# A transformer layer on one core: the order of all steps as a table, the last batch projected by head, the norms' roots as powers on POOL

## The reference

```
x = x + attn(layernorm(x))       # 16 heads, latent keys = values (72 wide), causal softmax,
                                 #   z[t, 16*72] @ out_w + out_b
x = x + birwkv(r = layernorm(x), k = v = ctx)
                                 # sigmoid(r) * (Af + Ab + cur*v) / (Bf + Bb + cur),
                                 #   A, B = forward and backward scans over the 128 tokens
x = x + moe(layernorm(x))        # 8 experts, top 2 of them per token, silu(x Wg) * (x Wu), then Wd
layernorm(x) = (x - mean) / sqrt(var + 1e-5)
```

## Time and profile before

| | us |
|---|---|
| median of 3 runs | 646.59 (645.44 to 647.18) |
| the profiled execution's own time | 645.62 |
| its span, from the first to the last instruction | 644.0 |
| PE busy | 549.7 (85%) |
| DVE busy | 427.3 (66%) |
| ACT busy | 367.4 (57%) |
| POOL busy | 341.5 (53%) |

### The profile page before, as it was taken

One profiled execution on the slowest core, in us unless ns is written; L12 is line 12 of the kernel. 1 busy time (PEld: TensorE's weight loads), 2 busy tenths in 40 slices (PEclk: granted clock), 3 DMA queues, 4 the chain that ended last, 5 costly groups with the idle time before them and its releaser, 6 DMA issues.

```text
span 644.0 us, 11145 instructions
## 1 busy us (share of the span) xinstructions
PE 549.7 (85%) x3714; PEld 480.9 (75%) x3714; DVE 427.3 (66%) x888; ACT 367.4 (57%) x995; POOL 341.5 (53%) x313
## 2 busy tenths in 40 slices
PE   1987688999898999999869757894799999999991
PEld 0875566778677888878648437784799999999991
DVE  4468485685888786846846858594477777777760
ACT  4276554676467765655553344563467667776750
POOL 3374757547372486623611742173766767665433
PEclk9999988999899999999878668797889999999997
DMA  6324444364354425443120277256668897888710
GB/s 208 126 47 71 61 86 62 51 84 74 56 98 85 70 44 74 95 88 61 44 92 22 93 224 256 61 113 187 155 155 238 221 237 204 230 224 224 174 28 0
DMA packets 54540, 76.04 MB, mean 118 GB/s; under 512 B 11410, under 2 KB 42899, under 8 KB 54227
## 3 DMA queue, kind: packets, MB, share of 16 engines
q1 hardware_dynamic: 43210, 63.32, 40.2%
q0 software_dynamic: 10384, 11.86, 9.7%
q10 hardware_dynamic: 888, 0.15, 0.1%
HBM read 49.03 MB, written 10.40 MB: 92 GB/s over the span
## 4 chain that ended last, share of the span: by engine, by line
PE 50%; DVE 16%; POOL 12%; issue 9%; ACT 7%; DMA 4%; SPq 0%; POOLq 0%; ACTq 0%; DVEq 0%
PE P L921 22%; PE PO L921 9%; PE PO L1031 5%; PE P L999 4%; PE P L1017 4%; POOL xs L1830 3%; ACT EB L1212 2%; POOL EB L1787 2%; DVE small L1450 2%; PE P L1007 2%; DVE ZT L1465 2%; DMA out<-Y,TK 1%; PE P L1069 1%; ACT XN L1173 1%; PE P L939 1%
## 5 line engine op out<-in xcount | busy, mean ns | idle before, releaser
L921 PE MATMUL P<-GT,WF 128*128 128x256 f32 x1104 | 149.3, 294 | 10.1 <-DVE GT L1362 6.0
L921 PEld LDWEIGHTS P<-GT,WF 128*128 128x128 f32 x1104 | 142.8, 201 | 11.3 <-DVE GT L1362 6.7
L1212 ACT ACTIVATE EB<-P,small 128x128 f32<-128x128 f32 x256 | 90.7, 367 | 97.1 <-DVE small L1450 96.9
L1787 POOL TENSOR_TENSOR EB<-EB,small 128x512 f32<-128x512 f32 x64 | 77.1, 1206 | 127.3 <-DVE small L1454 127.1
L1871 POOL DMA_INDIRECT out<-Y,TK x46 | 74.8, 1626 | 74.2 <-ACT Y L1301 56.3
L1017 PE MATMUL P<-PT,V 128*72 128x512 f32 x128 | 71.0, 639 | 18.0 <-DVE ZT L1465 16.6
L1844 POOL DMA_INDIRECT cxa<-xd,TK x46 | 62.2, 1353 | 39.7 <-DMA TK<-xs 29.0
L1031 PE MATMUL PO<-Ow,zP 128*128 128x256 f32 x288 | 73.4, 396 | 3.2 <-DMA zP<-ZT 1.9
L999 PEld LDWEIGHTS P<-KT,qT 72*128 72x128 f32 x512 | 68.9, 196 | 8.2 <-DMA qT<-qP 4.5
L999 PE MATMUL P<-KT,qT 72*128 72x128 f32 x512 | 69.6, 280 | 4.1 <-DMA qT<-qP 3.6
L921 PE MATMUL PO<-WF,HR 128*128 128x256 f32 x552 | 71.4, 287 | 0.0
(11 more groups left out here) (182 smaller groups left out, 930.9 us busy)
## 6 DMA issues: line engine op xcount, KB each, us to landing
WR<-wf SPq DMA_DIRECT2D x33, 512.0 KB, 4.9
arena<-wf SPq DMA_DIRECT2D x33, 512.0 KB, 5.0
qT<-qP SPq DMA_DIRECT2D x63, 128.0 KB
zP<-ZT SPq DMA_DIRECT2D x80, 72.0 KB
zP<-ZT SPq DMA_DIRECT2D x96, 36.0 KB
X<-x SPq DMA_DIRECT2D x4, 512.0 KB, 7.4
cxa<-ctxin SPq DMA_DIRECT2D x4, 512.0 KB, 6.8
out<-X SPq DMA_DIRECT2D x3, 512.0 KB, 4.3
```

The costliest lines, as they stand in the source:

```text
L921: r = e.matmul(o, lt(a), rt_(b), start=start and n == 0, stop=stop and n == 2, skip_group_check=skip)
L1212: e.activation(EB[i][:, j, :], S[:, 128 * j:128 * j + 128], ACT.Exp, bias=NM[i][:, j:j + 1], accum_out=SM[i][:, j:j + 1]).then_inc(s_exp, 1)
L1787: e.tensor_tensor(EB[i][:, :, :], EB[i][:, :, :], SM[i].unsqueeze(2).broadcast_to([128, 4, 128]), ALU.mult).then_inc(s_prob, 1)
```

## The change

Four things change together.

1. The planner is gone. ORDER is a table, STEPS, of words such as `S.5` or `rs.3.3.2.2`, up to tile 10; from there a loop emits the same pattern as before. Steps keep their content, but nearly all side steps move by some places. The output of a tile, on POOL, has a step of its own (`ao`) and no longer goes with `dn`.
2. The last batch (15) is not packed. SP loads a second copy of the output weights, ordered by head, into the query buffer 0 (`load_ow_by_head`, two DMAs, 1.18 MB), and `project_by_head` multiplies ZT with it: 4 matmuls of 72 rows after each of its four units, 16 in place of 9, in another quarter of the PSUM tensor PO.
3. All roots of the norms are one POOL instruction, `tensor_tensor(..., ALU.pow)` with -0.5. The 10 or 13 small operations go.
4. Waits that follow from the buffers: HR and the low half of the weights of tile 1, and the loads of tile 1, wait for the last projection.

```diff
-SHARE, SHARE_TILES = 0.7, 3.0
...
+STEPS = """
...
+S.63 Y.59 add.6 bn.2.3.0.0 ltk.3 agg.2.3.0.2 rs.2.3.0.2 N.62 N.63 T.60 gtk.0 Y.60 nr.3.0.2 sig.3.0.0 x2.3.0.0.1 gtk.1 O.14.0
...
+"""
-    def newton(kind, g, b0, nb, i):
...
             def pack_z(n):
                 k, b, hq = UNITS[n]
                 z, nb = packing(n)
-                if nb == 1 or b % NB == NB - 1:
+                if b < B - 1 and (nb == 1 or b % NB == NB - 1):
...
+            def load_ow_by_head():
+                sp.wait_ge(s_S, PER * (NK - 1))
+                by_head = ow.rearrange("p m c -> (p m) c").rearrange("(h l) c -> l h c", l=L)
+                e.dma_start(qT[0][:, 4:16, :], by_head[:, 0:12, :]).then_inc(s_owh, 16)
+                e.dma_start(qT[0][:, 0:4, :], by_head[:, 12:16, :]).then_inc(s_owh, 16)
...
+            def project_by_head(b, i):
+                n = 4 * b + i
+                buf, half, _ = z_home(n)
+                o = PO[:, 1, 256:512]
+                if i == 0:
+                    pe.wait_ge(s_owh, 32)
+                    pe.wait_ge(s_wk, total["wb"])
+                    pe.wait_ge(s_add, b // 2)
+                pe.wait_ge(s_z, n + 1)
+                for j in range(4):
+                    p = e.matmul(o, ZT[buf][:, j, 128 * half:128 * half + 128], ow_head(4 * i + j), start=4 * i + j == 0, stop=4 * i + j == H - 1)
+                p.then_inc(s_O, 1)
...
-                e.tensor_scalar(ve[:, 0:nb], mv[:, 0:nb, 1], EPS, -0.5, ALU.add, ALU.mult).then_inc(s_ve, 1)
+                e.tensor_scalar(ve[:, 0:nb], mv[:, 0:nb, 1], EPS, None, ALU.add).then_inc(s_ve, 1)
...
+            def rstd(kind, g, b0, nb):
+                y = rs1[:, GB * g:GB * g + GB] if kind == 1 else rs2
+                po.wait_ge(s_nhalf, 1)
+                po.wait_ge(s_ve, nth("agg", kind, g, b0, nb))
+                e.tensor_tensor(y[:, 0:nb], ve[:, 0:nb], nhalf[:, 0:nb], ALU.pow).then_inc(s_rstd, 1)
```

More of the change, by code:

```diff
@@ L73, in schedule @@
+tg.10 lw.12.1 sh.9.0 sh.9.1 lw.11.2 ao.7 sw.9.2 lxg.12
+"""
 def schedule():
-    order = []
+    order = [(name, *map(int, a)) for name, *a in (w.split(".") for w in STEPS.split())]
     def emit(*step):
[L78 to L241, removed]
@@ L272, in plan @@
[L272 to L291, removed]
@@ L318, in split_w @@
-    def split_w(j, k):
[L319 to L328, removed]
@@ L330, in turn @@
-    def turn(n, k=1):
-        for _ in range(k):
-            now[0] += 1
-            credit[0] = min(credit[0] + st["share"], st["share"] + 0.1)
-            for i, parts_ in enumerate(beside):
-                while credit[0] > 0 and parts_ and parts_[0][0] <= n and wake[i] <= now[0]:
-                    c = next(parts_[0][1], "end")
-                    if c == "end":
-                        parts_.pop(0)
-                    elif c is not None and c < 0:
-                        wake[i] = now[0] - c
-                    else:
-                        credit[0] -= c or 0.6
@@ L344, in finish @@
-    def finish(n, until):
-        st["rush"] = True
-        while not until():
-            assert any(p and p[0][0] <= n for p in beside)
-            for i, parts_ in enumerate(beside):
-                if parts_ and parts_[0][0] <= n and next(parts_[0][1], "end") == "end":
-                    parts_.pop(0)
-        st["rush"] = False
-    for p in (0, 2):
-        emit("bn", 1, 0, 0, p)
-    emit("agg", 1, 0, 0, GB, True)
-    for i in range(3):
-        emit("rs", 1, 0, 0, GB, i)
-    emit("nmb", 1, 0, 0, GB)
@@ L505, in schedule @@
-    for j in range(2, NT):
-        due = j + 1 < NT and not ready(j + 1)
-        def prepare(k):
-            if not due:
-                split_w(j + 1, k)
-        beside_turn(j + 3)
-        prepare(0)
-        product(j, 0)
-        beside_turn(j + 3)
-        if j + 1 < NT and not due:
-            emit("tg", j + 1)
-        beside_turn(j + 3)
-        prepare(1)
+        if step[1] < NT:
+            order.append(step)
+    def split_w(j, k):
+        emit("sw", j, k)
+        emit("lw", j + 2, k)
```

374 lines of the change are left out of this document (126 added, 248 removed).

## The result

The changed kernel takes 619.66 us (616.59 to 624.57, four runs), and the kernel before on the same chip 646.88 (645.44 to 647.82): a ratio of 0.9588, interval 0.9516 to 0.9661. On two more chips the same program gave 0.9683 (0.963 to 0.9737) and 0.9603 (0.9562 to 0.9645); taken together that is some 0.962, or 24 us. A few single executions ran slower at a lower granted clock, and the ratios leave them out. The profiled execution took 621.72 us, its span 620.0 against 644.0.

What follows compares the result with a forecast made beforehand. The prediction took PE's idle time in attention (33.6 us) and in the passage to the experts as the only room for gain. 645.62 - 14.2 (passage) - 5 (behind tile 5) - 8 (attention) = 618.4, said as 618, range 608 to 626.

Steps and rivals of the forecast that it cites:

- Attention, -8: Attention up to the last scores: 8 us saved, mostly by Newton roots leaving POOL, out of 33.6 us of PE idle time.
- near what the POOL roots hold: Basis of the attention estimate: Newton roots on POOL held about 6.5 us of the chain of waits.
- rival 1: Attention: the new order also packs it and three quarters of PE's idle time go, -25 us, 601 in all; chance 0.20.
- The passage, -14.2: Passage from attention to the experts: tile 5's transposes come at 435 us in place of 449.24, saving 14.2 us.
- the first weights set the pace: End of attention: group 2's first weights land at 370 us, 8 us of work follows, last add at about 378.
- Behind tile 5, -5: Behind tile 5's transposes: tile 6's wait of 4.58 us and most of 1.8 us of slow products go, saving 5.
- The power at 0.3 us: Norm roots: each becomes one POOL power instruction, taken at 0.3 us with its semaphores.
- the forecast's own sign, over 1 us: POOL's power in the profile after: the forecast counts as wrong if it takes over 1 us.
- Rival 4: Roots on POOL: the power is slow, 2.6 us each, costing 30 us, so 648 us, slower than before; chance 0.07.
- The power's first call: First power on POOL: might pay about 6 us once, with 2 us of cover, ending 4 us later.
- Rival 2: End of attention: late first weights hold ACT and DVE, add at 388 us, attention gains nothing, 632 in all; chance 0.21.
- Rival 3: Passage: tile 5's chain doesn't move, scatters still end near 430 us, 645 us in all; chance 0.05.

## Why the prediction was right in the time and wrong in its parts

618 was forecast, 619.66 measured, in the forecast's own range. That the order of the table makes the gain was right; its shares and two of its reasons were not.

- **Attention, -8, mostly by the roots.** It gave 17.1 us, and the roots alone are not its reason: powers in the old order move the last scores by 1 us. With the powers in both, the order moves them from 354.95 to 339.64. (Without the powers the new order was only run with blocks of Newton steps, which end attention at 359.84.) The failed step is "near what the POOL roots hold": I priced the removed instructions and had no price for the moved steps, though 33.6 us of idle time bounded it. 11.5 us of that went, between my -8 and rival 1. The other 5.6 us are PE's busy time up to the last scores. One unit's transposes and product with the values no longer stand ahead of them, some 2 us, and behind 300 us the granted clock is 0.95 in place of 0.87.
- **The passage, -14.2.** From the last scores it is -1.4. In parts: last scores to add 37.9 before, 23.5 forecast, 32.2 now; add to first scatter 29.0, 21 and 26.6; first scatter to tile 5's transposes 27.7, 36 and 34.6. The third is right to 1.4 us.

  The first failed in the path: I let the first weights set the pace. Nobody waits for them: POOL issues them by 354.12, they land in 3.7 to 4.9 us, and their split on DVE starts at 361.34, 23.9 us behind the last scores where I had 15.5. From the split to the add it takes 8.3 us, as I had it. What lies ahead of the split is the hole of 7.29 us, which no row of before shows, and then PE's own work: the profile's chain of waits goes through the packed projection of batch 14 (L718) and through three of the four pieces of the projection by head, 1.73 us each, of which I had counted only the last.

  The second part failed in its savings: the two roots take 0.8 and 1.7 us from variance to use, so they give 1.5 us and not 3.4, and the granted clock is 0.50 and 0.52 from 372.28 to 396 us, where it was 0.82 and 0.84 before from 392 to 422 us. The logits' 16 matmuls take 3.58 us for 1.95:

```profile
382.96 3.58 PE L734 MATMUL P<-small,XT 128*128 128x8 f32 x16 [0.47 <-ACT XT L873]
407.32 1.95 PE L1047 MATMUL P<-small,XT 128*128 128x8 f32 x16 [0.47 <-ACT XT L1184]
```

  The first row is from the changed kernel, the second from the kernel before.

  Yet with the powers the new order is needed in the passage: in the old one, with the powers in it, the section takes 103.6 to 105.9 us. The new order saves some 13 us there, and the powers in the old one cost 11, so against the kernel before hardly anything is left.
- **Behind tile 5, -5:** 5.6, as forecast; tile 6's wait of 4.58 us is 0.53.
- **The signs in absolute times** came out well by luck: first scatter 396.23 for 399, tile 5's transposes 430.82 for 435. They were counted with attention ending where it did before; it ended 17 us earlier, and the passage used that up.
- **The power at 0.3 us** takes 0.72 us on 128x2 and 1.07 on 128x4 in the mean. By the forecast's own sign, over 1 us, it should have failed. It did not: in the passage the table places the roots where little waits for them, 0.24 and 1.73 us on DVE for the last two, against 11.46 in the old order. Rival 4 named the right engine and the wrong price: its queue is the danger, not its arithmetic.
- **The power's first call** shows no gap but 2.28 us for DVE's variance, and takes as long as the next one (POOL's timeline). The 6 us that the Trainium skill (GPSIMD Engine Reference, 2.1 Instruction dispatch) gives for the first call of a freshly loaded kernel are not to be seen; whether a power is such a call, no run here shows.

```profile
7.25 1.05 POOL L1446 TENSOR_TENSOR small<-small 128x4 f32<-128x4 f32 x1 [2.28 <-DVE small L1090]
...
25.37 1.05 POOL L1446 TENSOR_TENSOR small<-small 128x4 f32<-128x4 f32 x1 [4.17 <-DVE small L1090]
```

- **Rival 2** occurred in part: DVE stood 3.64 us before the split of the first weights at 361.34, with copies into ZT behind it. But what held the split was not the weights: ScalarE's copy ahead of it waited 5.06 us for PE's transposes. **Rival 3** is out: the slots of tile 5 were loaded at 419.32, against 439.75.

The errors cancelled, and that is luck: 9 us too little in attention, 13 too much in the passage, 1 too little behind it. The time alone would have passed for proof of the whole working; only kernels with one part each, and the profile's sections, showed that one of its three terms had the wrong cause and another the wrong path.

## What to carry to other kernels

An instruction moved to another engine takes over that engine's queue: ask what stands ahead of it there and what that waits for, before you ask how long it takes. A cheaper instruction and the order that suits it are one change; tried alone in the old order, the powers (+0.7%) would have been thrown away, though the new order with blocks of Newton steps in their place is 5% slower (spread steps were not tried there). And where the idle time of a stretch is latency between engines, small work is priced by how it stands in the queue that all units pass through: in the old order 21 us of it on DVE, spread, cost attention about 1 us against the powers, and the same roots in blocks about 14.

## What the hardware showed that was not expected

A power on POOL takes 0.71 to 0.73 us for 128x2 and 1.02 to 1.05 for 128x4 (once 1.46), where a product of the same 128x4 shape took 0.20. And engines stood for up to 5.4 us with nothing in the trace that they wait for, in every kernel profiled here but the one before, within a few microseconds of the last scores or some 50 us ahead of them, at places that shifted with the program; what they wait for was not found.
